# A three-tile ring for the feature buffer, and block 0's hot items cut per tile, in a recommendation-model tower

## The reference

```python
e = jnp.stack([tbl_f[ids[:, f]] for f in range(26)], axis=1)      # (2048, 26, 128), abridged
combined = jnp.concatenate([e, r_dense_x[:, None, :]], axis=1)
interact = jnp.einsum('bfd,bgd->bfg', combined, combined)
z = interact[:, triu_i, triu_j]                                    # 351 pairs
h = jnp.concatenate([z, r_dense_x], axis=1)
h = jnp.maximum(h @ W_top1 + b_top1, 0.0)                          # 479 -> 512
h = jnp.maximum(h @ W_top2 + b_top2, 0.0)                          # 512 -> 256
y = h @ W_top3                                                     # 256 -> 1
```

## Time and profile before

| | |
|---|---|
| median of 3 runs | 480.82 us (480.33 to 482.65) |
| the profiled execution's own time | 486.82 us |
| its span in the trace | 485.0 us |
| PE busy | 437.1 us (90%), 3464 records |
| DVE busy | 310.4 us (64%) |
| ACT busy | 230.2 us (47%) |
| POOL busy | 247.8 us (51%), 256 gathers |
| DMA | 36.20 MB, mean 75 GB/s |

### The profile page before, as it was taken

One profiled execution on the slowest core, in us unless ns is written; L12 is line 12 of the kernel. 1 busy time (PEld: TensorE's weight loads), 2 busy tenths in 40 slices (PEclk: granted clock), 3 DMA queues, 4 the chain that ended last, 5 costly groups with the idle time before them and its releaser, 6 DMA issues.

```text
span 485.0 us, 9121 instructions
## 1 busy us (share of the span) xinstructions
PE 437.1 (90%) x3464; PEld 413.9 (85%) x3464; DVE 310.4 (64%) x503; ACT 230.2 (47%) x731; POOL 247.8 (51%) x264
## 2 busy tenths in 40 slices
PE   1776669899998999999889999999999999999978
PEld 1665669899897999999889998989898989889966
DVE  4998237875387735885469645885488745882441
ACT  2643343644455453644545444644546453634643
POOL 3652665655655556455654656555565556461000
PEclk9999679999999999999999999999999999999999
DMA  6789212322123312232122321232133312310000
GB/s 229 222 258 160 57 45 58 81 70 72 48 63 75 81 51 57 70 82 73 44 66 78 73 65 55 70 76 78 39 72 80 80 55 56 72 49 18 1 1 0
DMA packets 23995, 36.20 MB, mean 75 GB/s; under 512 B 6185, under 2 KB 18097, under 8 KB 23952
## 3 DMA queue, kind: packets, MB, share of 16 engines
q1 hardware_dynamic: 14880, 18.03, 14.7%
q0 software_dynamic: 8192, 16.79, 12.8%
q10 hardware_dynamic: 880, 0.80, 0.5%
HBM read 35.59 MB, written 0.01 MB: 73 GB/s over the span
## 4 chain that ended last, share of the span: by engine, by line
PE 82%; DMA 7%; issue 4%; POOL 3%; DVE 2%; ACT 0%; POOLq 0%; ACTq 0%; DVEq 0%
PE x_ps L418 31%; PE gram_ps L434 24%; PE tail_ps L489 15%; DMA raw<-in_tbl,ids_sb 7%; PE x_ps L405 5%; POOL raw L388 3%; PE tail_ps L468 3%; PE tail_ps L459 2%; PE tail_ps L495 2%; DVE gram L269 1%; DVE onehot L593 1%; DMA ids_sb<-in_ids 0%; DVE z L278 0%; ACT gram L269 0%; DVE zt_lo L326 0%
## 5 line engine op out<-in xcount | busy, mean ns | idle before, releaser
L388 POOL DMA_INDIRECT raw<-in_tbl,ids_sb x256 | 246.9, 964 | 190.9 <-DMA raw<-in_tbl,ids_sb 94.6
L593 DVE TENSOR_TENSOR onehot<-ids_wide,row_ps 128x1024 fp32r<-128x1024 int32 (+1 forms) x160 | 202.6, 1298 | 41.2 <-PE x_ps L418 32.3
L418 PE MATMUL x_ps<-onehot,hot_hi 128*128 128x256 f32 x688 | 180.1, 297 | 22.2 <-DVE onehot L593 20.2
L418 PE MATMUL x_ps<-onehot,hot_lo 128*128 128x256 f32 x688 | 171.4, 283 | 0.0
L418 PEld LDWEIGHTS x_ps<-onehot,hot_hi 128*128 128x128 f32 x688 | 131.3, 191 | 26.5 <-issue 11.9
L434 PE MATMUL gram_ps<-xt 128*128 128x108 f32 x1024 | 134.2, 284 | 7.3 <-DVE gram L269 5.8
L434 PEld LDWEIGHTS gram_ps<-xt 128*128 128x128 f32 x1024 | 126.9, 199 | 13.6 <-ACT gram L269 7.6
L418 PEld LDWEIGHTS x_ps<-onehot,hot_lo 128*128 128x128 f32 x688 | 131.6, 191 | 0.0
L269 DVE COPY gram<-gram_ps 32x104 f32<-32x104 f32 x256 | 68.6, 268 | 90.2 <-PE gram_ps L434 86.3
L269 ACT COPY gram<-gram_ps 32x104 f32<-32x104 f32 x256 | 60.2, 235 | 88.7 <-PE gram_ps L434 80.1
L530 ACT COPY xt<-x_ps 128x256 f32<-128x256 f32 x80 | 50.4, 633 | 50.1 <-PE x_ps L418 42.0
(11 more groups left out here) (36 smaller groups left out, 279.0 us busy)
## 6 DMA issues: line engine op xcount, KB each, us to landing
ids_wide<-in_hot_ids SPq DMA_DIRECT2D x80, 128.0 KB
raw<-in_tbl,ids_sb POOLq DMA_INDIRECT x256
hot_in<-in_tbl SPq DMA_DIRECT2D x7, 512.0 KB, 6.8
hot_in<-in_tbl SPq DMA_DIRECT2D x3, 640.0 KB, 6.6
dense_sb<-in_dense_t ACTq DMA_DIRECT2D x6, 128.0 KB
weights_in_place<-in_w SPq DMA_DIRECT2D x1, 512.0 KB
dense_sb<-in_dense_t SPq DMA_DIRECT2D x2, 128.0 KB
weights_in_place<-in_w SPq DMA_DIRECT2D x1, 256.0 KB
```

The lines of the kernel that those rows point to most:

```text
L388: nc.gpsimd.indirect_dma_start(out=raw[k][:, f, :], out_offset=None, in_=tables[f], in_offset=bass.IndirectOffsetOnAxis(ap=ids_sb[:, t, f: ...
L418: last = nc.tensor.matmul(ps, table[:, chunk_at[j] + c, :], onehot[:, p % RING, c - a, :], start=(c == 0 and table is hot_hi), stop=(c == ...
L593: nc.vector.tensor_tensor(onehot[:, p % RING, 0:n, :], ids_wide[:, it % IDS, :].unsqueeze(1).to_broadcast([P, n, BLOCK]), row_no[chunks[it ...
```

## The change

`xt` becomes a ring of three tiles (XT = 3, 384 samples), so that the next block's first tile can be filled while a tile is still in use. The items of block 0 are cut per tile, 10 for tile 0 and 10 for tile 1, each of 128 columns instead of 256. Block 0's order becomes: the items and turns of tile 0, then the 8 gram steps of tile 0 with a piece of tile 1's items behind each, the rest of tile 1's items and its turns, then 8 gram steps in a row. For later blocks the order is: one item of the next block, the 8 grams of the first tile in a row, about half of the next block's items with the turns of the second tile, the 8 grams of the second tile in a row, the other items with the turns of the next tile. The tail of a block is spread from the end of its own grams to the second gram run of the next block. In blocks 2 to 7 its layer `h1` thus comes between the gram steps of a first tile.

Pieces are at most 4 chunks of 256 columns (8 of 128), so a table of 10 chunks has three pieces in blocks 1 to 7. The number of pieces goes from 160 to 187. Before a gram run DVE makes no piece, and after a gram step at most one. LOADS_AHEAD is 2, and SP issues the ids of four items of tile 1 before the weights, which are rounded at gram steps 11 to 15 of block 0. An item that wraps around the ring is copied to `xt` in two halves.

```diff
-PIECE = 5
-EARLY = 2
+PIECE = 4
+XT = 3
+ROUNDS_AHEAD = 2
-LOADS_AHEAD = 3
+LOADS_AHEAD = 2
...
-    items = blocks * nh
+    items = [(j, t, 1) for t in range(tiles_block) for j in range(nh)]
+    items += [(j, h * tiles_block, tiles_block) for h in range(1, blocks) for j in range(nh)]
...
+        if h == 0:
+            second = hot_pieces(1)
+            slots += gram_slots(t, second[:n_gram])
+            rest_slots = second[n_gram:]
+            slots += with_turn(rest_slots, t + 1, item_ends(rest_slots))
+            lead = 0
+        elif hot:
+            held = item_end[pieces[hot[0][0][1]][0]] - hot[0][0][1]
+            slots += hot[:held] + gram_slots(t)
+            slots[-1].append(("held", pieces[hot[0][0][1]][0]))
+            lead = item_end[pieces[hot[len(hot) // 2][0][1]][0]] - hot[0][0][1]
+            ends = item_ends(hot[held:lead])[:-1]
+            slots += with_turn(slots[-1:] + hot[held:lead], t + 1, [0] + [end + 1 for end in ends])[1:]
+            tail_to.append(len(slots))
...
+        slots += gram_slots(t + 1)
+        tail_from.append(len(slots))
+        if hot:
+            rest_slots = hot[lead:]
+            slots += with_turn(rest_slots, t + tiles_block, item_ends(rest_slots))
...
             end = min(used + RING + 1, len(pieces))
+            coming = [s[0] for s in order[n + 1:] if s[0] in ("gram", "hot")][:1]
+            if step[0] == "gram":
+                end = min(end, nxt + 1)
+            elif coming == ["gram"]:
+                end = nxt
...
-        xt = sb("xt", [P, BLOCK, SLOTS])
+        xt = sb("xt", [P, XT * P, SLOTS])
...
+        weights_at_gram = range(gram_block - len(weight_parts), gram_block)
...
+        def to_xt(copy, first, n, feature, src):
+            at = first % XT
+            runs = [(0, n)] if at + n <= XT else [(0, XT - at), (XT - at, n)]
+            for a, b in runs:
+                place = (first + a) % XT * P
+                last = copy(xt[:, place:place + (b - a) * P, feature], src[:, a * P:b * P])
+            return last
...
-                if j == EARLY:
-                    dense_load(0)
+            dense_load(0)
+            for it in range(nh, nh + IDS):
+                ids_load(it)
```

More of the change, by code:

```diff
@@ L105, in build @@
     item_start = [0] + item_end[:-1]
[L107 to L118, removed]
-            stage_ends = part == parts[key[0]] - 1 and key[1] == tail_count[key[0]] - 1
[L120 to L144, removed]
@@ L146, in build, with hot_pieces, with_turn @@
-    first_steps = hot_steps(0, item_end[EARLY - 1])
-    order = first_steps + [step for h in range(blocks) for step in plan(h)]
+    last_item = [max(it for it, (_, first, n) in enumerate(items) if first <= t < first + n) for t in range(tiles)]
+    def hot_pieces(t):
+        of = [p for p, (it, _, _) in enumerate(pieces) if items[it][1] == t]
+        return [[("hot", p)] for p in of]
+    def with_turn(slots, t, ends):
+        for g in range(n_turn):
+            slots[ends[-(-(g + 1) * len(ends) // n_turn) - 1]].append(("turn", t, g))
+        return slots
@@ new lines, in build @@
+    held_items = [step[1] for slot in slots for step in slot if step[0] == "held"]
+    for h in range(blocks - 1):
+        at = COVER_START
+        span = [at]
+        for key, part in tail_steps[:-1]:
+            stage_ends = part == parts[key[0]] - 1 and key[1] == tail_count[key[0]] - 1
+            at += COVER_STAGE if stage_ends else COVER[key[0]]
+            span.append(at)
+        n = tail_to[h] - tail_from[h]
+        before = {}
+        for (key, part), at in zip(tail_steps, span):
+            before.setdefault(tail_from[h] + min(int(at * n / span[-1]), n - 1), []).append(("tail", h, key, part))
+        for i, steps in before.items():
+            slots[i][:0] = steps
@@ L148, in build @@
+    order = [step for slot in slots for step in slot]
     fills = [("hot", pieces[s[1]][0]) if s[0] == "hot" else s for s in order
@@ L154, in pieces_made @@
         made, nxt, used = [], 0, -1
-        for step in order:
+        for n, step in enumerate(order):
             if step[0] == "hot":
@@ L363, in _ @@
                 dense_load(h)
-            for it in range(nh, items):
+            for it in range(nh + IDS, len(items)):
                 ids_load(it)
@@ L417, in hot_piece @@
                     for table in (hot_hi, hot_lo):
-                        last = nc.tensor.matmul(ps, table[:, chunk_at[j] + c, :], onehot[:, p % RING, c - a, :],
+                        last = nc.tensor.matmul(ps, table[:, chunk_at[j] + c, :], columns(p)[:, c - a, :],
                                                 start=(c == 0 and table is hot_hi),
@@ L525, in hot_copy @@
             def hot_copy(it):
-                h, j = divmod(it, nh)
+                j, first, n = items[it]
                 act.wait_ge(piece_used, item_end[it])
@@ L586, in make_piece @@
                 it, a, b = pieces[p]
+                j, _, tiles_item = items[it]
+                width = tiles_item * P
                 if p == item_start[it]:
```

95 lines of the change are left out of this document (53 added, 42 removed).

## The result

The changed kernel took 512.88 us (median of 4 runs, 512.78 to 513.65), the kernel before 481.74 beside it (4 runs, 480.33 to 486.86): 1.063 times before, interval 1.055 to 1.071. The forecast was 485.9 in a range of 473 to 498. The profiled execution has a span of 511.0 us, before 485.0.

The account below looks back on a forecast made before the run. PE was taken as the bound from 84 us on, gathers then PE before. Mark +4.0 and waits after it +1.1 gave +5.1 on 486.8, so 491.9, times 0.988: 485.9 us, range 473 to 498.

Parts of the forecast that it names:

- I take 0.112: 19.3 us: Tile 1 of block 0: 172 hot matmuls of 128 columns at 0.112 us each, 19.3 us, within 10.3 to 37.0.
- the mark: Point where block 0's 16 grams and two block 1 items are done: 84.5 us before, forecast at about 88.
- the other terms of that sum (copy wait, one-hot, weights): First gram to mark, 43.5 us: included PE waits of 0.7 for ACT's copy, 0.6 for DVE's one-hot, 1.3 for weights.
- the gathers' gain: Tile 0: weights issued later let the 16th gather go at 37.5 us, not 41.82; first gram at 44.0, not 49.0.
- rival 4: Overlap fails: first gram stays at 49, new work all added, +5.0 more, 491 us; chance counted within the forecast's 0.53.
- +1.1: Net change of PE's waits after the mark, all blocks' terms together: 1.1 us longer.
- +2: After the mark: gram runs of eight have no slack for DVE's late copy signals; 2 us more, between 0 and 12.
- `zt`'s waits: After the mark: waits of `zt` for the copies of `cols`, 2.9 us, would shrink by 2.5, at worst 0.
- the term of the one-hot behind the first step: Second-tile gram runs, blocks 1 to 6: DVE's one-hot delays a gram copy, 6 x 0.6 = 3.6 us more.
- Rival 1: Short hot matmuls in block 0 cost 0.215 us each, tile 1 +17.7 and tile 0 +5: 508 us; chance 0.15.
- Rival 2: Faster: first gram at 40.5 us, gram runs without dearer signals, one-hot hidden: 475.3 us; chance 0.24.
- Rival 3: 128-column matmul quicker than its weight load looks, 0.081 us, tile 1 5.3 us less: 480.7 us; chance 0.08.

Follow-up runs that it names:

- short at the upper level: Kernel after with table 0's tile 0 item streamed twice and 84 filling 256-column matmuls ahead of tile 0's last turn: 504.36 us, 1.045 of before.
- columns doubled: Kernel after, each of block 0's 344 hot matmuls streaming its 128 one-hot columns twice: 489.43 us, 1.029 of before.
- before with its weights later: Kernel before, MLP weights fetched behind item 13's ids and tile 1's last turn, rounded and split behind grams 11 to 15: 1.013 of before.
- block 4: Kernel after with block 0 in whole items, block 4's 172 hot matmuls each cut into two of 128 columns: 505.38 us, 1.035 of before.
- filled wait: Kernel after, tile 0's hot matmuls streaming columns twice, 84 filling 256-column matmuls ahead of tile 0's last turn, tile 1 short: 502.31 us, 1.024 of before.
- before with short halves: Kernel before, each of block 0's 172 hot matmuls cut into two of 128 columns, nothing else: 495.80 us, 1.044 of before.
- the late versions: Kernel before plus 350 or 175 filling 256-column matmuls (42 or 21 us) ahead of tile 0's last turn: 505.03 us (1.045) and 484.75 us (1.007).
- doubled in tile 0 only: Kernel after, only tile 0's ten items streaming their columns twice, tile 1's 172 hot matmuls kept at 128 columns: 511.79 us, 1.077 of before.

## Why the prediction was wrong

**The step that failed** is the price of the 172 short hot matmuls, "I take 0.112: 19.3 us", together with "A granted clock near 1.00 there instead of 0.76": the stage from the first gram to the mark was priced at the upper level of PE's clock and ran at the lower. The mark moved by 37.1 us, not 4.0. 172 x (0.213 - 0.112) = 17.4 us; the first eight gram steps 8 x (1.78 - 0.94) = 6.7; the 48 records of the second run 8.16 - 48 x 0.112 = 2.8; four turns 4 x (0.89 - 0.44) = 1.8. That is 28.7 us; the stage took 26.8 more than the 43.5 forecast. With the level at its upper value throughout (short at the upper level) it took 43.8, so the other terms of that sum (copy wait, one-hot, weights) stand as a whole.

**Tile 0.** The first gram came at 51.2, not 44. PE's 172 short matmuls at 0.213 alone are 36.6 us, PE came to the last turn at 49.69, and the chain holds no gather: the 16th had been issued at 39.78 us, ahead of the weights (43.78). With PE free (columns doubled) the first gram came at 51.1 as well. There the weights went out at 37.73, as forecast, but the group of three ahead of the 16th gather met them, not only the last table, and the 16th was issued at 43.75 us, not 37.5. So the gathers' gain would not have come either, which is what rival 4 had as its condition (a first gram at 49 or later). That the weights hold gathers up is shown by before with its weights later, with 1.44 us in place of 5.07; even there the first gram came at 47.0, not 44.

**After the mark.** +1.1 was forecast, and -11.1 came out in the first pair, beyond the 6 us at which the prediction calls itself wrong. With both kernels on one chip it is +0.3. The 400.5 us belong to the first trace of before: the 5.8 us of waits for DVE's copies, from which a +2 was worked out, are not there in the second. PE's waits in after from 84 to 465 us, against the earlier trace rows, are these two and no more:

```profile
PE gram_ps L482 <- DVE gram L317: 3.7, 8, 0.8
PE gram_ps L482 <- ACT xt L604: 0.7, 1, 0.7
```

The forecast had the waits for DVE's copies above 5.8 us; they are 3.7. It had `zt`'s waits near nothing, and they are gone. Six of the eight waits are 0.45 or 0.46 us and stand in the second-tile runs of blocks 1 to 6, like this one:

```profile
177.52 4.80 PE L482 MATMUL gram_ps<-xt 128*128 128x108 f32 x40 [0.45 <-DVE gram L317]
```

That is the term of the one-hot behind the first step, 2.7 us instead of 3.6; the rest of the +1.1 is not shown term by term.

**The rivals.** Rival 1 came nearest in time (508), with the chance of 0.15, and that is partly luck, since its mechanism fell: a short fp32r matmul takes 0.112 at the upper level. Its argument was a pair of rows in which 256-column matmuls stood 0.21 apart at 11 us. The same pair was the sign of the lower level, and the question to ask was what raises the level and whether the new stream does. Rival 2 needed a first gram at 40.5 us; no kernel had one before 47.0. Rival 3 (0.081, which is two fifths of the way from 0.06 to 0.112, not a third) is out: 0.112 in three kernels. The Trainium skill, page "TensorE: Matmul & The Clock Gate", section "Back-to-back issue gap", has about 81 ns for a sustained matmul of this width with its weight load; these traces have 112 ns for fp32r data, and the measurement decides. The Trainium skill, same page, section "LDWEIGHTS (loading the stationary operand)", puts a weight load at its columns divided by 1.2 in ns, which for 128 columns gives an estimate of 107 ns. The 112 ns at the upper level agree with it, the 213 ns at the lower do not.

**Why the cost of +37 us at the mark shows as 26 to 38 us in all.** Against the first trace of before 11 us came back, which was that trace's own; against the second (mark 88.0, span 477.0) the mark is 34.0 later and the span 34.3 longer. In before's own order 21 us of extra PE work ahead of the first gram are nearly free (+2.9), since PE otherwise waits for gathers in tile 1's stage; after filled that slack and went 34 us beyond the old mark.

What stays open: why short matmuls held the upper level in block 4 and, in short at the upper level, in tile 1, and lost it in tile 0 of that kernel and in tile 1 of filled wait. The two losses followed waits of 0.56 and 0.95 us, and where the level held no wait stood among them, but no run changed the waits alone. Open is also why before with short halves has 381.4 us behind its mark on one chip and the late versions 393.2 on another. Even with the level mostly up, the change did not pay: columns doubled and filled wait stand 2 to 3% above before. No version tried beat the kernel before.

## What to carry to other kernels

Halving the moving columns of these fp32r matmuls, from 256 to 128 with 128 weight columns, saved next to nothing on each (0.112 against 0.119 us) and doubled their count. Worse, in the kernel after PE stayed at the lower level of its clock until all of them were done (to 111 us), and everything beside them took twice as long. In a start phase ask first at which level the rows stand, and what there could raise it. Before a stage's gain or loss is added to the total, look for the waits behind it that a shift would absorb, and take a second trace of the same kernel before a difference of 2% is explained.

## What the runs showed of the hardware

PE can be busy without a gap and stay at the lower level: with 128-column fp32r matmuls it did for 36.00 of 36 us (spacing 0.213), and at a recorded 0.50 for 23.81 of 24 us. The level rose behind stretches of 256-column ones (5.7 us of them in columns doubled, 3 us of filling in short at the upper level) and of grams without short matmuls between them (5 us, to 110 us in doubled in tile 0 only). The Trainium skill, page "TensorE: Matmul & The Clock Gate", section "What's actually happening", lets the clock depend on how busy PE has been. The traces here agree only in part: from 22 to 46 us PE was busy for 14.68 of 24 us at 0.95 in columns doubled, and for 23.81 of 24 at 0.50 in short at the upper level.

Streaming every column of block 0 twice made the kernel faster: 512.88 to 489.43 us (4.6%, on different chips), 1.063 or 1.087 to 1.029 of before. The scatter of executions also differs: before had 468.7 to 482.8 us on one chip (13 runs), after 513.15 to 513.55 beside it.
